# Cross attention on 32 batches: where the operand x is transposed, and how many operand tiles it uses

## The chip, the cores and the metric

One core of a Trainium2 chip runs the whole kernel. The metric is the device time of one execution in microseconds. Before the change the median of three runs is 336.96 us (336.56 to 337.16).

## The reference

Two layers run over 32 batches of x and y (the context), each 128 channels by 1024 positions.

```
# layer 0, per batch, 8 heads of 16 channels, softmax over a head's 16 channels
att(q, k, v) = v @ softmax(q.T @ k * 16**-0.5)            # per head, q, k, v are projections
x1 = x + y + proj_p2r @ att(wq_rgb x, wk_point y, wv_point y)
           + proj_r2p @ att(wq_point y, wk_rgb x, wv_rgb x)
# layer 1, per batch, 8 heads
q, k = Wq y + bq, Wk y + bk ;  v = Wv x1 + bv
o    = Wo (softmax(q k.T / sqrt(128)) v) + bo + x1        # attention between channels of a head
out  = (o - mean(o)) / sqrt(var(o) + 1e-5) * gn_w + gn_b  # mean and variance over the whole batch
```

All attention is between channels, so each batch needs only the 128x128 Gram matrices y y', y x' and the row sums of y; everything up to the normalisation is then one pair of 128x128 matrices P and Q with out = P x + Q y + shift.

## The kernel before, in words

The batches are taken in pairs (b = 0, 1); `h` counts two pairs, `u` is the pair in it, `p = 2h + u` is the number of the pair, and `slot = 2u + b` names one of four buffers. A batch passes three stages, and `step(h, u, front, middle, back, post)` does one stage each for three pairs: *front* builds the Gram of pair p, *middle* turns the Gram of pair p-1 into P and Q, *back* applies the P and Q of pair p-2 to its x and y, and *post* normalises pair p-3. `steps` calls it for 18 values of p: four by hand, twelve in a hardware loop of two steps (VectorE has its last two of these by hand), and the last two, one without front and one without front and middle. Each engine has its own list of calls in this step, and order on an engine is that of its list; semaphores alone tie the engines together.

Front. The operand tile `t` (four of them, `TB = 4`, one a slot) holds, for eight chunks of positions, y transposed (128 columns), a column of ones, and x transposed (128 columns). In the loop VectorE writes y from `y_blocks` by 32x32 block transposes (`y_transpose`, two halves a batch), and x of the second batch of a pair from `x_blocks` (`x_transpose` of VectorE). The x of the first batch is transposed by TensorE (`x_transpose` of PE, two groups of four into the banks `tpx`), and ScalarE copies it out (`xt_out`). The first four batches are all transposed on TensorE (`x_transpose_early`, `y_transpose_early`); ScalarE and VectorE copy them out. `gram_chunks` multiplies, ScalarE copies (`gram_out`), VectorE mirrors the part that was not computed (`gram_mirror`).

Middle. `u12_products` and `u3_products` multiply the Gram with key and query weights into `mid0` and `mid1`; ScalarE (`u12_out`, `keys_times_sums`) and VectorE (`u3_out`) copy out; `scores` fills six 32-column blocks of `mid0`; softmax alternates between VectorE (`shift_scores`, `softmax_out`) and ScalarE (`exponent`); `z_products`, `z_out` and `m_products` give `nmat` (`n12_out`, `n3_out` on VectorE), `pq_products` gives P and Q in `mid1`. Attention times bv is made in `softmax_out` by three VectorE operations and multiplied with Wo in `m_products` into two columns, from which `c_out` makes the shift. In the list of TensorE `pq_products(p - 2)` stands behind the first group of x transposes.

Back. The output product runs with split operands: `pq_hi` (ScalarE, `pq_high`) and `pq_lo` (VectorE, `pq_low`, from the bank and `pq_hi`), and `xy_hi` (ScalarE, `split_high`) and `xy_lo` (GpSimd, `split_low`, four pieces of 256 columns for x and for y). `out_half` sums hi*hi, hi*lo (parts 0) and lo*hi (parts 1) for x and y into `oacc`; ScalarE copies it out (`out_to_sbuf`), VectorE takes statistics (`half_stats`, `half_moments`, `partition_moments`, `variance`), TensorE averages over partitions (`group_moments`), GpSimd raises to the power -1/2 (`deviation`), ScalarE makes scale and shift and normalises (`norm_scale`, `normalise`), and issues the store. All loads are issued by SP, in its order: `refill_blocks` when both transposes of a batch are done, `refill_raw` when `xy_hi` and `xy_lo` are, each for the batch two pairs later.

In the last but one step ScalarE's list has the two `split_high` of the last batch, then `norm_scale(p - 3)`, and only then the first `out_to_sbuf`, and PE's product for the next use of `oacc` waits for that copy. `keep_warm` fills PE's pauses there with products that nobody reads.

Of the kernel before, what the change touches and what calls it, by code (L numbers as in the profile page):

```python
# [6 lines left out]
B, C, N, H = 32, 128, 1024, 8  # L7
EPS = 1e-5
# [4 lines left out]
QUADS = 4  # L13
# [4 lines left out]
TB = 4  # L18
# [6 lines left out]
VNAMES = ["bq", "bo", "gn_w", "gn_b"]  # L25


def cross_attention_pair_kernel(nc, x, y, weights, vectors, quad_rows, consts, out):
# [13 lines left out]
    with ctx:  # L42
# [14 lines left out]
        bk32, bv32 = quad[:, 0, :], quad[:, 1, :]  # L57
# [5 lines left out]
        zero_eps = cst[:, k0:k0 + 4]  # L63
# [5 lines left out]
        def col(name):  # L69
            k = VNAMES.index(name)  # L70
            return vec[:, k:k + 1]
# [5 lines left out]
        x_blocks = [sb(f"x_blocks{n}", [C, QUADS, N // QUADS]) for n in range(2)]  # L77
# [15 lines left out]
        abv_m = sb("abv_m", [C, 2, W32])  # L93
        square = sb("square", [C, 2])
        gmean = sb("gmean", [C, 2])
        gsquare = sb("gsquare", [C, 2])
        gvar = sb("gvar", [C, 2])
        abv = sb("abv", [C, 2])
# [4 lines left out]
        pq_lo = [sb(f"pq_lo{n}", [C, 2, 2, C], f32r) for n in range(2)]  # L103
        gate = sb("gate", [1, 10])
# [16 lines left out]
        sc = mid0[:, 0:6 * W32].rearrange("p (i c) -> p i c", c=W32)  # L121
        probs = mid0[:, 6 * W32:12 * W32].rearrange("p (i c) -> p i c", c=W32)
        stat_mb = stat[:, 0:4].rearrange("p (m b) -> p m b", b=2)
        pstat = stat[:, 8:12].rearrange("p (b m) -> p b m", m=2)
        mean_s, abv_s = stat[:, 16:18], mid0[:, 12 * W32:12 * W32 + 2]
        gacc_b = [gacc[:, 0:GW], stat[:, H64:H64 + GW]]
        oacc = [pb(f"oacc{n}", [C, HALF]) for n in range(2)]
        o_last = [oacc, [gacc, mid1]]
        y_early = [oacc, [mid0, mid1], oacc, oacc]
# [3 lines left out]
        weights_in = sem("weights_in")  # L133
        x_in = [sem(f"x_in{n}") for n in range(4)]
        y_in = [sem(f"y_in{n}") for n in range(4)]
        blocks_in = [sem(f"blocks_in{n}") for n in range(4)]
        x_blocks_in = [sem(f"x_blocks_in{n}") for n in range(2)]
# [3 lines left out]
        prepared = sem("prepared")  # L141
        attn_zero = sem("attn_zero")
# [23 lines left out]
        abv_step = sem("abv_step")  # L166
        abv_ready = sem("abv_ready")
# [5 lines left out]
        wo_abv_done = sem("wo_abv_done")  # L173
# [3 lines left out]
        pqhi_ready = sem("pqhi_ready")  # L177
        pqlo_ready = sem("pqlo_ready")
# [7 lines left out]
        square_ready = sem("square_ready")  # L186
# [4 lines left out]
        gvar_ready = sem("gvar_ready")  # L191
# [31 lines left out]
        def _(sp):  # L223
# [12 lines left out]
            def load_x_blocks(h, u):  # L236

                blocks = x[4 * h + 2 * u + 1].rearrange("(i c) (a m) -> a c i m", c=W32, a=QUADS)
                for a in range(QUADS):
                    sp.dma_start(x_blocks[u][W32 * a:W32 * (a + 1), :, :], blocks[a]).then_inc(x_blocks_in[u], 16)  # L240
# [14 lines left out]
            for n in range(2, 4):  # L255
                load_x(0, n)
                load_y(0, n)
# [940 lines left out]
```

## Time and profile before

| | |
|---|---|
| runs | 336.56, 336.96, 337.16 us |
| profiled execution | 336.94 us; its span, first to last instruction, 335.2 us |
| busy | PE 313.4, VectorE 263.8, ScalarE 231.2, GpSimd 190.4 us |
| moved | 56.8 MB read, 16.8 MB written |

The span is what the engines do; some 1.7 us of the time lie around it. Busy shares are averages over a start, thirteen alike steps and an end, so the stages have to be read one by one.

### The profile page before, as it was taken

How to read it: one execution, taken by the hardware profiler on the slowest of the kernel's cores; microseconds unless marked ns; L12 is line 12 of the kernel's file. 1: busy time of each engine (PE TensorE's matmuls, PEld its weight loads, DVE VectorE, ACT ScalarE, POOL GpSimd, SP SyncE). 2: the span in 40 equal slices, each digit the busy share in tenths (PEclk: the TensorE clock that was granted, in tenths of full speed). 3: DMA queues.
4: the chain of work that ended last, by engine and by line, in shares of the span. 5: the costliest groups of instructions: out<-in, count | busy, mean ns of one | idle time of the engine just before them, and what ended most of it. 6: DMA issues, size and time to landing. Idle time of an engine off the chain costs nothing.

```text
span 335.2 us, 12612 instructions
## 1 busy us (share of the span) xinstructions
PE 313.4 (94%) x4808; PEld 273.0 (81%) x4808; DVE 263.8 (79%) x716; ACT 231.2 (69%) x382; POOL 190.4 (57%) x277
## 2 busy tenths in 40 slices
PE   6999999999978999999999999999999999994980
PEld 3887898989866898988888898989898888972760
DVE  1595888988985788888898889888888999653574
ACT  3653757878785787878787797878787878954332
POOL 0874482757676275767667575757676675754010
PEclk9999999999999999999999999999999999997897
DMA  7999989498989949797998989797979670300215
GB/s 224 389 258 300 261 230 245 162 276 225 284 230 299 232 123 285 226 297 214 305 244 251 283 210 319 195 298 217 287 221 299 174 250 1 125 0 22 105 47 204
DMA packets 39061, 73.88 MB, mean 220 GB/s; under 512 B 4608, under 2 KB 26368, under 8 KB 39040
## 3 DMA queue, kind: packets, MB, share of 16 engines
q1 hardware_dynamic: 35008, 58.92, 64.6%
q10 hardware_dynamic: 4032, 14.68, 12.2%
q8 instruction: 13, 0.21, 0.3%
q14 instruction: 8, 0.07, 0.1%
HBM read 56.81 MB, written 16.78 MB: 220 GB/s over the span
## 4 chain that ended last, share of the span: by engine, by line
PE 88%; issue 3%; DVE 2%; POOL 2%; DMA 2%; ACT 2%; SPq 0%; POOLq 0%; ACTq 0%
PE oacc L429 10%; PE oacc L436 9%; PE oacc L430 9%; PE mid L526 5%; PE mid L454 4%; PE gacc L391 4%; PE mid L503 4%; PE stat L393 4%; PE tpx L348 4%; PE gacc L392 3%; PE gacc L393 3%; PE stat L392 3%; PE stat L391 3%; PE mid L512 2%; PE gacc L409 2%
## 5 line engine op out<-in xcount | busy, mean ns | idle before, releaser
L1129 POOL TENSOR_TENSOR xy_lo<-raw,xy_hi 128x256 fp32r<-128x256 f32 x256 | 179.9, 740 | 116.5 <-ACT xy_hi L696 116.5
L696 ACT ACTIVATE xy_hi<-raw 128x1024 fp32r<-128x1024 f32 x64 | 66.9, 1048 | 0.0
L856 DVE STREAM_TRANSPOSE t<-y_blocks 128x512 f32<-128x512 f32 x56 | 62.9, 1162 | 0.0
L429 PE MATMUL oacc<-xy_hi,pq_hi 128*128 128x512 f32 x124 | 55.6, 448 | 5.0 <-ACT res L703 4.8
L885 DVE BATCH_NORM_STATS2 hstat<-res 128x6 f32<-128x512 f32 x60 | 40.1, 688 | 22.8 <-ACT res L703 22.7
L703 ACT ACTIVATE res<-oacc 128x512 f32<-128x512 f32 x60 | 35.6, 594 | 30.7 <-PE oacc L436 30.4
L430 PE MATMUL oacc<-xy_lo,pq_hi 128*128 128x512 f32 x124 | 50.0, 403 | 1.5 <-issue 1.5
L394 PE MATMUL gacc<-t 128*32 128x225 f32 x224 | 45.4, 354 | 0.0
L393 PE MATMUL gacc<-t 128*32 128x225 f32 x224 | 45.4, 354 | 0.0
L394 PE MATMUL stat<-t 128*32 128x225 f32 x224 | 44.9, 353 | 0.0
L393 PE MATMUL stat<-t 128*32 128x225 f32 x224 | 44.9, 353 | 0.0
L391 PE MATMUL stat<-t 128*32 128x129 f32 x224 | 43.0, 272 | 1.8 <-issue 1.8
L392 PE MATMUL gacc<-t 128*32 128x161 f32 x224 | 44.2, 300 | 0.0
L392 PE MATMUL stat<-t 128*32 128x161 f32 x224 | 43.9, 299 | 0.0
L391 PE MATMUL gacc<-t 128*32 128x129 f32 x224 | 43.1, 273 | 0.4 <-issue 0.3
L436 PE MATMUL oacc<-xy_hi,pq_lo 128*128 128x512 f32 x124 | 40.9, 411 | 0.0
L717 ACT ACTIVATE res<-res,nbias,nscale 128x1024 f32<-128x1024 f32 x29 | 36.0, 1241 | 4.8 <-issue 4.3
L395 PE MATMUL stat<-t 128*32 128x96 f32 x224 | 36.8, 246 | 0.0
L395 PE MATMUL gacc<-t 128*32 128x96 f32 x224 | 36.8, 246 | 0.0
L429 PEld LDWEIGHTS oacc<-xy_hi,pq_hi 128*128 128x128 f32 x124 | 23.8, 192 | 12.8 <-issue 7.6
L866 DVE STREAM_TRANSPOSE t<-x_blocks 128x512 f32<-128x512 f32 x28 | 31.9, 1139 | 0.0
L396 PE MATMUL gacc<-t 128*32 128x64 f32 x224 | 30.8, 219 | 0.0
(146 smaller groups left out, 916.8 us busy)
## 6 DMA issues: line engine op xcount, KB each, us to landing
raw<-in_x SPq DMA_DIRECT2D x31, 512.0 KB, 5.7
raw<-in_ctx SPq DMA_DIRECT2D x31, 512.0 KB, 7.0
y_blocks<-in_ctx SPq DMA_DIRECT2D x112, 128.0 KB, 7.0
out<-res ACTq DMA_DIRECT2D x28, 512.0 KB, 3.4
x_blocks<-in_x SPq DMA_DIRECT2D x56, 128.0 KB, 6.7
out<-res SPq DMA_DIRECT2D x4, 512.0 KB, 2.8
wt<-in_weights SPq DMA_DIRECT2D x1, 896.0 KB, 7.0
raw<-in_x SPq DMA_DIRECT2D x2, 256.0 KB, 3.7
```

What stands on the lines that cost most here:

```text
L391: pe.matmul(acc[0:W32, C:GW], wa, tb[:, c, C:GW], start=first, stop=False)
L392: pe.matmul(acc[3 * W32:C, 3 * W32:GW], wd, tb[:, c, 3 * W32:GW], start=first, stop=False)
L393: pe.matmul(acc[W32:H64, W32:GW], wb, tb[:, c, W32:GW], start=first, stop=final)
L394: pe.matmul(acc[H64:3 * W32, W32:GW], wc, tb[:, c, W32:GW], start=first, stop=final)
L395: pe.matmul(acc[0:W32, 0:3 * W32], wa, tb[:, c, 0:3 * W32], start=False, stop=final)
L429: pe.matmul(bank[:, :], whi, xy_hi[slot][:, s, cols], start=(s == 0), stop=False)
L430: pe.matmul(bank[:, :], whi, xy_lo[slot][:, s, cols], start=False, stop=False)
L436: mm = pe.matmul(bank[:, :], pq_lo[u][:, b, s, :], xy_hi[slot][:, s, cols], start=False, stop=(s == 1))
L696: act.activation(xy_hi[slot][:, s, :], raw[slot][:, s, :], ACT.Copy).then_inc(split_hi, 1)
L856: dve.transpose(dst, blocks[:, HC * i:HC * (i + 1)]).then_inc(yt_ready, 1)
L885: dve.bn_stats(hstat[:, b, half, :], res[2 * u + b][:, half * HALF:(half + 1) * HALF])\
L1129: piece = pool.tensor_tensor(xy_lo[slot][:, s, cols], raw[slot][:, s, cols], xy_hi[slot][:, s, cols].bitcast(f32), ALU.subtract)
```

## The change

Every x of the loop is transposed by VectorE from `x_blocks` (now four tiles, loaded for every batch), and so is batch 3 at the start, x and y. Only two operand tiles are left, one for each b, so the halves of a batch's transposes spread around the mirror and into the next step. The TensorE banks `tpx` then hold u12, u3, the scores and the exponents, `mid` holds z, M and P, Q alone. The low parts of P and Q are made by GpSimd from SBUF, for which ScalarE copies the bank a second time (`pq_copy`). Attention times bv is no longer made on VectorE: z of Wo times bv are two one-column products. The chain of mean and variance is written in scalar-pointer forms. In the loop PE computes the high parts of both first halves ahead of the low parts. The last two steps have new lists on all engines: P and Q of the last pair are made one step earlier, ScalarE's scale of the older pair comes behind all copies, outputs go to four more banks, and `keep_warm` stands in one place only.

```diff
-TB = 4
+TB = 2
-        x_blocks = [sb(f"x_blocks{n}", ...) for n in range(2)]
+        x_blocks = [sb(f"x_blocks{n}", ...) for n in range(4)]
+        pq_full = sb("pq_full", [C, 2, 2, C])
+        tail = [tpx[i].rearrange("p m r -> p (m r)") for i in range(2)]
+        u12_bank, u3_bank = tail[0], tail[1][:, 0:2 * C]
+        sc = tail[1][:, 2 * C:2 * C + 6 * W32].rearrange("p (i c) -> p i c", c=W32)
+        probs = tail[0][:, 0:6 * W32].rearrange("p (i c) -> p i c", c=W32)
+        o_next = [oacc, [gacc, oacc[0]]]
+        o_last = [tail, [oacc[1], gacc]]
# SP
             def refill_blocks(h, u, b):
                 n = 4 * h + 2 * u + b
                 sp.wait_ge(yt_ready, 2 * n + 2)
                 load_blocks(h + 1, 2 * u + b)
-                if b == 1:
-                    sp.wait_ge(xt_ready[1], n + 1)
-                    load_x_blocks(h + 1, u)
+                sp.wait_ge(xt_ready[b], n - b + 2)
+                load_x_blocks(h + 1, 2 * u + b)
# TensorE, out_half
-                if half == 0 and b == 0:
-                    pe.wait_ge(pqlo_ready, 2 * h + u + 1)
+                if half == 0:
+                    pe.wait_ge(pqlo_ready, 2 * (2 * h + u) + b + 1)
# TensorE, z_operands
                 pe.wait_ge(attn_ready, p + 1)
+                if not (isinstance(p, int) and p < 1):
+                    pe.wait_ge(c_ready, p)
+                    pe.wait_ge(pq_copied, p)
# TensorE, m_products
-                pe.wait_ge(abv_ready, p + 1)
-                pe.matmul(mid0[:, 2 * C:2 * C + 2], w("oT"), abv[:, :], start=True, stop=True)
+                for a in range(2):
+                    mm = pe.matmul(mid0[:, 2 * C + a:2 * C + a + 1], z[:, a, 2, :],
+                                   (col("bv"), col("bv", vec_rot))[a], start=True, stop=True)
# TensorE, step in the loop
-                    x_transpose(h, u, 0)
                     pq_products(p - 2)
-                    x_transpose(h, u, 1)
                     u12_products(p - 1)
-                    out_half(h - 1, u, 0, 0)
                     u3_products(p - 1)
+                    out_half(h - 1, u, 0, 0, parts=(0,))
+                    out_half(h - 1, u, 0, 1, parts=(0,))
+                    out_half(h - 1, u, 0, 0, parts=(1,))
+                    out_half(h - 1, u, 0, 1, parts=(1,))
                     if post:
                         group_moments(p - 3)
-                    out_half(h - 1, u, 0, 1)
                     scores(p - 1)
# TensorE, last but one step (whole)
+                    u12_products(p - 1)
+                    u3_products(p - 1)
+                    pq_products(p - 2)
+                    scores(p - 1)
+                    out_half(h - 1, u, 0, 0, parts=(0,))
+                    out_half(h - 1, u, 0, 1, parts=(0,))
+                    out_half(h - 1, u, 0, 0, parts=(1,))
+                    out_half(h - 1, u, 0, 1, parts=(1,))
+                    z_operands(p - 1)
+                    keep_warm(1)
+                    z_products(p - 1)
+                    out_half(h - 1, u, 1, 0, banks=o_next, bank_free=0)
+                    group_moments(p - 3)
+                    m_products(p - 1, True)
+                    out_half(h - 1, u, 1, 1, parts=(0,), banks=o_next, bank_free=2 * n + 3)
+                    pq_products(p - 1)
+                    out_half(h - 1, u, 1, 1, parts=(1,), banks=o_next)
# ScalarE
+            def pq_copy(p):
+                if not (isinstance(p, int) and p < 1):
+                    act.wait_ge(pqlo_ready, 2 * p)
+                act.activation(pq_full[:, :, :, :], mid1[:, :], ACT.Copy).then_inc(pq_copied, 1)
# ScalarE, step in the loop (whole, "post" calls included)
+                    pq_high(p - 2, u)
+                    pq_copy(p - 2)
+                    u12_out(p - 1)
+                    keys_times_sums(p - 1)
+                    split_high(h - 1 + u, 1 - u, 1, 0, post)
+                    out_to_sbuf(h - 1, u, 0, 0)
+                    out_to_sbuf(h - 1, u, 0, 1)
+                    split_high(h - 1 + u, 1 - u, 1, 1, post)
+                    norm_scale(p - 3)
+                    exponent(p - 1)
+                    normalise(*before(h, u), 0)
+                    store(*before(h, u), 0)
+                    normalise(*before(h, u), 1)
+                    gram_out(p, 0)
+                    split_high(h, u, 0, 0, back)
+                    store(*before(h, u), 1)
+                    gram_out(p, 1)
+                    z_out(p - 1)
+                    split_high(h, u, 0, 1, back)
+                    out_to_sbuf(h - 1, u, 1, 0)
+                    out_to_sbuf(h - 1, u, 1, 1)
# ScalarE, last but one step (whole)
+                    u12_out(p - 1)
+                    keys_times_sums(p - 1)
+                    pq_high(p - 2, u)
+                    pq_copy(p - 2)
+                    split_high(h - 1, 1, 1, 0, True)
+                    exponent(p - 1)
+                    split_high(h - 1, 1, 1, 1, True)
+                    out_to_sbuf(h - 1, u, 0, 0)
+                    out_to_sbuf(h - 1, u, 0, 1)
+                    z_out_last(p - 1)
+                    out_to_sbuf(h - 1, u, 1, 0, o_next)
+                    pq_high(p - 1, 1 - u)
+                    pq_copy(p - 1)
+                    out_to_sbuf(h - 1, u, 1, 1, o_next)
+                    norm_scale(p - 3)
+                    normalise(*before(h, u), 0)
+                    store(*before(h, u), 0)
+                    normalise(*before(h, u), 1)
+                    store(*before(h, u), 1)
# ScalarE, last step (whole)
+                    norm_scale(p - 3)
+                    normalise(h - 1, 0, 0)
+                    normalise(h - 1, 0, 1)
+                    norm_scale(p - 2, slice(0, 1))
+                    normalise_last(h - 1, u, 0, range(2))
+                    normalise_last(h - 1, u, 1, range(1))
# VectorE, partition_moments and variance
+                for b in range(bs.start, bs.stop):
+                    mean = mom[:, 0, b:b + 1]
+                    last = dve.scalar_tensor_tensor(out=mom[:, 1, b:b + 1], in0=mean, scalar=mean,
+                                                    in1=pstat[:, b, 1:2], op0=ALU.mult, op1=ALU.add)
...
# VectorE, step in the loop (whole, "post" and "ahead" calls included)
+                    half_stats(*before(h, u), 1, 1)
+                    half_moments(p - 3)
+                    partition_moments(p - 3, 1 - u)
+                    u3_out(p - 1)
+                    x_transpose(h, u, 0, 1)
+                    y_transpose(h, u, 1, 0)
+                    x_transpose(h, u, 1, 0)
+                    variance(p - 3, 1 - u)
+                    shift_scores(p - 1)
+                    y_transpose(h, u, 1, 1)
+                    x_transpose(h, u, 1, 1)
+                    softmax_out(p - 1)
+                    half_stats(h - 1, u, 0, 0)
+                    half_stats(h - 1, u, 0, 1)
+                    y_transpose(h + u, 1 - u, 0, 0)
+                    x_transpose(h + u, 1 - u, 0, 0)
+                    gram_mirror(p)
+                    y_transpose(h + u, 1 - u, 0, 1)
+                    half_stats(h - 1, u, 1, 0)
+                    n12_out(p - 1)
+                    n3_out(p - 1)
+                    c_out(p - 1, 1 - u)
# GpSimd
+            def pq_low(p, parity):
+                pool.wait_ge(pqhi_ready, p + 1)
+                pool.wait_ge(pq_copied, p + 1)
+                for b in range(2):
+                    pool.tensor_tensor(pq_lo[parity][:, b, :, :], pq_full[:, b, :, :],
+                                       pq_hi[parity][:, b, :, :].bitcast(f32), ALU.subtract).then_inc(pqlo_ready, 1)
...
                 if middle and back:
+                    pq_low(p - 2, u)
                     split_low(h - 1 + u, 1 - u, 1, 0)
...
                 elif middle:
                     deviation(p - 3)
+                    pq_low(p - 1, 1 - u)
                     deviation(p - 2)
```

In the last step VectorE's variance of the last batch still waits for `norm_ready`, which ScalarE's `norm_scale(p - 2, slice(0, 1))` now raises.

## Rows read from the trace of the kernel before

**Rows 1.** The page: span, busy time and share by engine.
```profile
span 335.2 us, 12612 instructions
...
PE 313.4 (94%) x4808; PEld 273.0 (81%) x4808; DVE 263.8 (79%) x716; ACT 231.2 (69%) x382; POOL 190.4 (57%) x277
```

**Rows 2.** Windows (stretch, length, busy by engine, granted clock, DMA share, GB/s).
```profile
184.35:202.73 18.38, 18.38 (x317) 16.41 (x316) 16.22 (x43) 14.46 (x24) 11.85 (x18) 1.00 0.95 260
20.00:40.00 20.00, 19.70 (x211) 16.53 (x213) 14.50 (x32) 11.83 (x20) 8.63 (x14) 1.00 1.09 276
302.30:307.00 4.70, 0.00 (x0) 0.00 (x0) 0.07 (x1) 1.54 (x5) 3.09 (x5) 0.93 0.00 0
307.00:322.00 15.00, 14.42 (x85) 11.63 (x86) 9.60 (x33) 5.62 (x9) 0.03 (x1) 0.79 0.18 71
```

**Rows 3.** Timeline of VectorE in one pair: start, length, instruction, idle before it.
```profile
164.31 0.69 DVE L885 BATCH_NORM_STATS2 hstat<-res 128x6 f32<-128x512 f32 x1 [0.26 <-ACT res L703]
...
168.37 0.68 DVE L878 TENSOR_TENSOR pq_lo<-mid,pq_hi 128x512 fp32r<-128x512 f32 x1
168.97 2.28 DVE L856 STREAM_TRANSPOSE t<-y_blocks 128x512 f32<-128x512 f32 x2
...
172.50 1.12 DVE L866 STREAM_TRANSPOSE t<-x_blocks 128x512 f32<-128x512 f32 x1
...
176.54 0.36 DVE L981 TENSOR_REDUCE ssum<-mid 128x6 f32<-128x192 f32 x1 [0.81 <-ACT mid L659]
```

**Rows 4.** Timeline of the end: rows of GpSimd, PE and VectorE.
```profile
299.18 5.56 POOL L1129 TENSOR_TENSOR xy_lo<-raw,xy_hi 128x256 fp32r<-128x256 f32 x8 [4.11 <-ACT xy_hi L696]
...
307.04 0.77 PE L429 MATMUL oacc<-xy_hi,pq_hi 128*128 128x512 f32 x1 [4.78 <-ACT res L703]
...
317.47 1.16 PE L526 MATMUL mid<-nmat 128*128 128x128 f32 x8
...
316.99 0.42 DVE L1011 TENSOR_TENSOR nmat<-mid,cst 128x256 f32<-128x256 f32 x1
...
331.21 0.81 DVE L950 TENSOR_SCALAR res<-mid,nscale,nbias 128x512 f32<-128x512 f32 x1
```

**Rows 5.** Timeline of PE in one pair.
```profile
165.26 0.28 PE L517 MATMUL mid<-abv,wt 128*128 128x2 f32 x2
...
165.95 0.60 PE L348 MATMUL tpx<-cst,raw 128*128 128x128 f32 x4
166.39 1.06 PE L526 MATMUL mid<-nmat 128*128 128x128 f32 x8
...
167.72 1.03 PE L454 MATMUL mid<-wt,gram 128*128 128x256 f32 x4
168.42 0.57 PE L429 MATMUL oacc<-xy_hi,pq_hi 128*128 128x512 f32 x1
...
169.98 0.61 PE L463 MATMUL mid<-wt,gram 128*128 128x128 f32 x4
```

**Rows 6.** One line's instructions (min, median, max ns), and VectorE's timeline at the start.
```profile
L989 DVE TENSOR_TENSOR sinv<-sinv,own_half x16: 159/161/661, 25.3 to 309.7; 128x12 f32<-128x12 f32 x16
...
14.51 0.22 DVE L827 TENSOR_SCALAR wt<-wt 128x128 f32<-128x128 f32 x1
14.64 0.76 DVE L828 TENSOR_SCALAR wt<-wt 128x128 f32<-128x128 f32 x1
```

**Rows 7.** Timeline of GpSimd in the same pair.
```profile
179.11 1.44 POOL L1129 TENSOR_TENSOR xy_lo<-raw,xy_hi 128x256 fp32r<-128x256 f32 x2 [2.41 <-ACT xy_hi L696]
```

**Rows 8.** Windows of one microsecond each, columns as in rows 2, and issues to landing.
```profile
192.00:193.00 1.00, 1.00 (x40) 1.00 (x33) 0.93 (x5) 0.54 (x2) 1.00 (x3) 1.00 1.13 184
201.00:202.00 1.00, 1.00 (x8) 0.92 (x7) 0.90 (x2) 0.06 (x1) 1.00 (x3) 1.00 1.01 407
...
x_blocks<-in_x SPq DMA_DIRECT2D x56, 128.0 KB, 6.7
```

**Rows 9.** Timeline of PE: one of the two places where it waits for instructions.
```profile
107.96 0.50 PE L430 MATMUL oacc<-xy_lo,pq_hi 128*128 128x512 f32 x1 [1.54 <-issue]
```

More of the change, by code:

```diff
@@ L136, in cross_attention_pair_kernel @@
         blocks_in = [sem(f"blocks_in{n}") for n in range(4)]
-        x_blocks_in = [sem(f"x_blocks_in{n}") for n in range(2)]
+        x_blocks_in = [sem(f"x_blocks_in{n}") for n in range(4)]
         x_half_in = [sem(f"x_half_in{n}") for n in range(2)]
@@ L254, in _ @@
             sp.dma_start(w_rot[H64:C, :, :], weights[0:H64, k:k + 2, :]).then_inc(weights_in, 16)
[L255 to L257 removed]
+            load_x(0, 2)
+            load_y(0, 2)
+            sp.dma_start(vec_rot[0:H64, :], vectors[H64:C, :]).then_inc(weights_in, 16)
+            sp.dma_start(vec_rot[H64:C, :], vectors[0:H64, :]).then_inc(weights_in, 16)
+            load_blocks(0, 3)
+            load_x_blocks(0, 3)
             load_blocks(1, 0)
+            load_x_blocks(1, 0)
+            load_x(0, 3)
+            load_y(0, 3)
             load_blocks(1, 1)
[L260 removed]
+            load_x_blocks(1, 1)
             def raw_free(h, u, b):
@@ L408, in gram_full_width, with out_half @@
                 for c in range(begin, end):
-                    mm = pe.matmul(gacc_b[b], t[n][:, c, 0:C], t[n][:, c, :], start=(c == 0), stop=(c == CH - 1))
+                    mm = pe.matmul(gacc_b[b], t[b][:, c, 0:C], t[b][:, c, :], start=(c == 0), stop=(c == CH - 1))
                 if end == CH:
                     mm.then_inc(gram_done, 1)
-            def out_half(h, u, b, half, last=False, parts=range(2)):
-                bank = o_last[b][half] if last else oacc[half]
+            def out_half(h, u, b, half, parts=range(2), banks=(oacc, oacc), bank_free=None):
+                bank = banks[b][half]
                 slot = 2 * u + b
@@ L424, in out_half @@
                         pe.wait_ge(split_lo, 2 * n + 2)
-                    if not (last and b == 1):
+                    if bank_free is None:
                         pe.wait_ge(o_out, 2 * n + 1 + half)
+                    elif bank_free:
+                        pe.wait_ge(o_out, bank_free)
                     for s in range(2):
@@ L820, in _, with prepare_mask, prepare_weights @@
             dve.wait_ge(attn_zero, 2 * QUADS)
-            def prepare():
+            def prepare_mask():
+                s1 = float(C) ** -0.5
                 dve.wait_ge(consts_in, 16)
-                dve.wait_ge(weights_in, 80)
+                dve.wait_ge(small_in, 32)
+                dve.tensor_scalar(nbq[:, :], col("bq"), s1 * N, None, ALU.mult).then_inc(mask_ready, 1)
+                dve.tensor_copy(mask6[:, 0:4, :], other_head.unsqueeze(1).broadcast_to([C, 4, W32]))
+                dve.wait_ge(mask_ready, 1)
+                for a in range(2):
+                    last = dve.scalar_tensor_tensor(out=mask6[:, 4 + a, :], in0=bk32, scalar=nbq[:, :],
+                                                    in1=other_head, op0=ALU.mult, op1=ALU.add)
+                last.then_inc(mask_ready, 1)
+            def prepare_weights():
+                dve.wait_ge(weights_in, 16 * 5)
                 s0, s1 = float(C // H) ** -0.5, float(C) ** -0.5
@@ L1022, in step @@
                 if front and not middle:
-                    for b in range(2):
-                        for i in range(2):
-                            y_early_out(b, i)
-                    prepare()
+                    y_early_out(0, 0)
+                    y_early_out(0, 1)
+                    prepare_mask()
+                    y_early_out(1, 0)
+                    y_early_out(1, 1)
+                    prepare_weights()
                     gram_mirror(p)
```

285 lines of the change are left out of this document (100 added, 185 removed).

## The prediction

> **What bounds the kernel now.** I read the page first: TensorE is busy 94% of a 335.2 us span, VectorE 79% [rows 1]. Then the stretches: one pair of batches in the loop takes 18.38 us (18.40 in the pair before), with PE busy for all of it at the full granted clock (1.00, the 2.4 GHz level), VectorE 16.2, ScalarE 14.5, GpSimd 11.9 and a DMA share of 0.95 [rows 2]. So in the loop the bound is TensorE. The timeline of VectorE shows three idle pieces in a pair, from 0.26 to 0.81 us, 1.65 in all [rows 3], so it is occupied for 18.40 - 1.65 = 16.75. It is the next bound, 1.65 behind. The third view is the end: for 4.7 us PE does nothing, and in the 15 us after it the granted clock is 0.79 [rows 2]. PE waits there for a copy of ScalarE into res, which is queued behind the scale of an older pair, which waits for GpSimd's power, which stands behind 5.56 us of low parts [rows 4].
>
> **The change, part by part.** Times are of the profiled execution: 335.2 us span, 336.94 us run, so 1.74 us lie around the span; the median of the runs is 336.96, the same.
>
> PE, per pair in the loop. Two groups of four transposes of x go, 166.39 - 165.95 = 0.44 each, 0.88 together. The 2-column product (0.14, 165.26 to 165.40) becomes two products: +0.14. The first two output halves run in one row and switch once less: about -0.15 (the first product after a change of kind takes 0.57 where the others take 0.40) [rows 5]. PE needs 18.40 - 0.88 + 0.14 - 0.15 = 17.5.
>
> VectorE, per pair. It gains two transposes of x: one takes 1.12, of which the next instruction overlaps 0.08, so about +2.10. It loses the low part of P and Q, 0.60 (168.37 to 168.97). The mean and variance chain loses two operations and two waits, about -0.35. No trace shows the new scalar-pointer forms on two values; the nearest two-value operations are 0.07 apart without a wait and 0.19 with one, so the pair of them lies between 0 and +0.25; I take the first. The three operations for bv cost 0.10 of the softmax, since the chain sum, reciprocal, scale paces it [rows 3]. Trimmed of the ends of instructions that now overlap the next (six, 0.08 each) VectorE needs 16.75 + 2.10 - 0.60 - 0.35 - 0.10 - 0.50 = 17.3.
>
> But VectorE and PE now wait for each other in a ring. Before, x transposes stood in front of the P and Q products and covered the wait for nmat. Now: the last nmat addition starts, 0.48 later the first P/Q product runs (316.99 to 317.47 [rows 4]); 0.89 + 0.70 + 0.65 = 2.24 after that u3's product has landed (166.39, 167.72, then 0.65 as 169.98 to its reader) [rows 5]. In these 2.72 us VectorE has only 1.84 of work (end of nmat and shift 0.47, the last statistics 0.73, moments 0.31, partition moments 0.33) and idles for 0.88. From u3_out to the last nmat addition it has 15.4 without a pause: u3_out 0.48, eight transposes 8.6, variance 0.60, scores 1.04, softmax 1.3, three statistics 1.8, mirror 0.97, first nmat addition 0.64. Ring: 2.72 + 15.4 = 18.14. PE's 17.5 is inside it with 0.6 to spare, so TensorE stops being the bound and most of the 0.88 is lost.
>
> One more term. The scale of the softmax, two SBUF inputs, took 0.16 in most pairs and 0.66 in a few; the same 128x128 scaling took 0.22 in front of GpSimd's low parts and 0.76 beside them [rows 6]. In the loop it fell into GpSimd's pause (176.70 to 179.11 [rows 7]). Now GpSimd's second block of four low parts starts about 1.4 later in the pair, because the new low parts of P and Q (two of 0.74, as the 128x256 form of the page) and the later deviation precede it; it ends 10.5 us after the P/Q products, and the scale comes at 10.3. Bounds 0 to +0.5, I take +0.2. The Trainium skill (SBUF — State Buffer, "SBUF: two separate sides") says that GpSimd and a VectorE operation with two SBUF inputs exclude each other for a whole instruction, while a one-input operation doesn't wait. By that rule the transposes stay at their price, which the trace agrees with (1.07 to 1.22 us), and the scale pays up to one GpSimd piece; by a rule that made every VectorE operation wait, the pair would be over 20 us.
> So a pair takes 18.14 + 0.2 = **18.34**, against 18.40.
>
> ScalarE loses two copies of 0.49 and gains one of 0.50; it finishes z about 15.0 after the P/Q products, and PE asks at 15.1. Near, but PE has 0.6 in hand. The low parts of P and Q are ready at 3.0 (high copy 1.1 to 1.6, second copy to 2.2, GpSimd 0.74), and PE, with the high products of both halves first, asks at 4.0. Cost 0; without that order PE would wait about 0.4. Two operand tiles: t[0] is rewritten after this pair's first Gram (done at 8.8; VectorE comes at 12.2), t[1] for the pair itself at 4 to 9.7, needed at 10.4. Cost 0, with 0.6 of cover on the second.
>
> DMA: each pair loads 0.52 MB more in 1 KB runs. A microsecond with blocks alone moved 184 GB/s, one of raw or stores 407 [rows 8]: 0.52 / 0.184 = 2.85 us more on about 16.3 busy, 19.1 in all against 18.34. But loads are issued two pairs ahead and land in 7 us [rows 8]: some 20 us of lead, of which 12 pairs would use 12 x 0.8 = 10. I take 0; the bounds are 0 and, with no lead, +0.8 a pair.
>
> Start. Four early transposes groups of batch 3 (1.75 on PE) go, but its two x and two y transposes (4.3) stand on VectorE between softmax steps. By its durations the second half of batch 3 is ready at 28.7; then z 0.8, the Gram's rest 1.4 and the copy of z: the P/Q products start at 34.15, against 33.62 now: +0.5. Step to the next one: 52.0 against 52.3.
> Loop. Twelve pairs: 52.0 + 12 x 18.34 = 272.1. PE stood twice for instructions, about 1.8 and 2.0 us [rows 9], once in the run; of these 3.8 the cover of 0.9 hides part: +2.9. That makes 275.0, against 276.9: **-1.9**. Last full step: 17.5 against 18.0: **-0.5**.
>
> End. From the end of that step E (now 294.92) the span has 40.3 us left. In the new order nothing stands in front of the copies: u12, u3 and P/Q to 2.2, scores 2.9, the two halves to 5.9, z at 6.2 (softmax of the last pair done at 6.0), out and M to 10.1, last P/Q 11.9, high copy 12.7, second copy 13.2, low part 13.95; last outputs to 19.0. With no idle piece over 0.5 us PE keeps 2.4 GHz: the products that took 0.43 take 0.23. Then ScalarE is last: copy to 13.7, scale 14.7, two normalisations with stores 17.6, scale 19.0, two more 21.4 (1.24 each), scale of the last pair 22.2; VectorE's variance of the last batch waits for that, 0.4 + 0.82 + 0.50 to the last normalisation at 23.9; from there to the end 4.0 (331.21 to 335.2) [rows 4]. 27.9 in all: **-12.4**.
>
> Sum: -1.9 - 0.5 - 12.4 = -14.8; span 320.4, time **322**.
>
> **Rivals.**
> A longer ring. All eight transposes at their longest (1.22) beside GpSimd and the full 0.5 for the scale: 18.95 a pair, 12 x 0.6 = +7: **329**. For it: GpSimd is busier now. Against: one-input operations show little spread.
> A shorter ring. The trimmed durations are too long or the u3 wait is met earlier, and PE stays the bound at 17.6 to 17.7: 12 x -0.7 = -8: **314**. For it: VectorE's own work is 17.3. Against: the 2.24 us are three products in a row.
> The end gains half. Some copy on ScalarE holds PE, the clock falls to 1.2 GHz again, and 6 of the 12.4 come back: **328**. For it: it is one queue with 12 long activations. Against: GpSimd's power no longer has anything behind it that PE needs.
> The DMA queues decide, on the other side. Place: the loop; 0.95 x 18.38 = 17.5 engine-us a pair plus 2.85 x 1.13 = 3.2 make 20.7 at a share of 1.0. If the lead doesn't carry it, 12 x 2.4 = +28: **350**, slower. It decides from 18.34 + 14.9/12 = 19.6 a pair. Against: 20 us with mixed loads ran at a share of 1.09 [rows 2].
>
> **How the numbers follow.** Forecast 0.55 (its own range 317 to 327), longer ring 0.16, shorter ring 0.12, half the end 0.12, DMA 0.05. The range 314 to 329 leaves out about 2 in 10. A difference of 0.2% (0.7 us) is about what runs of this kernel can tell. Faster: all but the DMA case and a sliver of unlucky sums, 0.93; same 0.02; slower 0.05.
>
> **What would show it.** PE idle about 0.9 us in each pair, just before the P/Q products, released by nmat on VectorE; pair period 18.2 to 18.5; VectorE busy near 17.3 with one idle piece before u3_out; the softmax scale at 0.3 or more; in the end no PE idle piece over 1 us before 305, clock at its full level to the last products, and ScalarE's scale as the releaser of the last variance. A PE without idle in the loop, or raw and blocks awaited by ScalarE or VectorE, would make me wrong there.

## The result: slower, 341.6 us against 336.8

After the change the median of four runs is 341.6 us (340.1 to 343.3); the kernel before, run beside it, took 336.8 (336.05 to 337.16). The ratio is 1.0147, 95% interval [1.0084, 1.021]: slower by 0.8 to 2.1%. Some executions of any of these kernels are a few per cent longer at a lower granted clock; the medians in this document are of all runs, the ratios leave those executions out. The profiled execution took 340.34 us with a span of 338.3, where the prediction had 322 and 320.4: 17.9 us of span are to be explained.

The page of the kernel after (answers to [rows 1]; then slices of 8.5 us, granted clock and DMA share in tenths; then the loads and the instruction fetches by queue):

```profile
span 338.3 us, 12492 instructions
...
PE 304.0 (90%) x4696; PEld 262.1 (77%) x4696; DVE 277.9 (82%) x671; ACT 226.3 (67%) x371; POOL 214.3 (63%) x309
...
PEclk9999997989999999999999999999999999999996
DMA  7999999997889987999999999999999994311036
...
q1 hardware_dynamic: 44384, 67.32, 73.8%
...
q8 instruction: 12, 0.20, 0.3%
```

PE was busy 9.4 us less and the span grew by 3.1. The clock dips in slices 7 and 9, in the first steps, and no longer between 302 and 322 us, where it had dipped before [rows 2]; it falls again only in the last slice, when PE has almost nothing left to do. A yardstick for the place of the loss is the start of the last nmat addition, once a step, here in us (before, line 1011; after, line 1002):

| | 1st | 2nd | 3rd | 4th | 5th | 14th | 15th | span end |
|---|---|---|---|---|---|---|---|---|
| before | 33.14 | 51.58 | 69.79 | 88.21 | 110.46 | 276.01 | 294.44 | 335.2 |
| after | 34.30 | 58.64 | 81.80 | 100.62 | 122.21 | 290.80 | 309.48 | 338.3 |

From row to row: the start +1.2; the first four steps 87.9 instead of 77.3, +10.6; nine steady steps 168.6 (18.73 each) instead of 165.55 (18.39), +3.0; the last full step +0.25; the end 28.8 instead of 40.8, -11.9. Together +3.1.

**The first steps.** PE's timeline of the kernel after, the three longest waits for which the profile names no releaser ("issue"), as in [rows 9]:

```profile
52.11 1.09 PE L494 MATMUL mid<-wt,attn 64*64 64x128 f32 x17 [4.14 <-issue]
...
72.97 0.37 PE L381 MATMUL stat<-t 128*32 128x96 f32 x1 [3.30 <-issue]
...
114.86 0.35 PE L380 MATMUL stat<-t 128*32 128x225 f32 x1 [2.99 <-issue]
```

Windows of the same kernel, columns as in [rows 2]:

```profile
52.00:56.00 4.00, 3.89 (x24) 3.02 (x24) 0.00 (x0) 2.68 (x4) 0.00 (x0) 0.57 1.12 236
...
50.00:60.00 10.00, 7.88 (x48) 6.30 (x48) 3.14 (x6) 3.87 (x5) 2.81 (x4) 0.83 1.08 262
...
70.00:80.00 10.00, 7.03 (x88) 6.23 (x89) 6.04 (x11) 5.48 (x8) 2.80 (x4) 0.83 1.07 337
```

With 1.37 and 0.48 us earlier, PE stood 12.3 us in such waits between 20 and 122 us; in the kernel before 3.6. Around the waits at 52 and 73 us the granted clock falls from 2.4 to 1.2 GHz: 0.57 in the row 52:56 means 3.4 of the 4 us at the lower level. It doesn't fall behind the wait of 2.99 us. No engine covers such a gap: VectorE is busy 3.14 us of ten.

What PE waits for can be read from the trace's DMA packets. The instruction queue q8 moves 12 packets of 16 KB in the run (0.20 MB by the page), and one belongs to each long wait:

| PE stands | packet begins | packet has landed | PE goes on | landing to going on |
|---|---|---|---|---|
| 47.97 | 49.43 | 50.51 | 52.11 | 1.60 |
| 69.67 | 70.22 | 71.66 | 72.97 | 1.31 |
| 111.87 | 112.06 | 113.38 | 114.86 | 1.48 |

In each row the packet begins only after PE has stopped. The 13 profiles of this document hold 51 such waits of 0.3 us or more between 40 and 122 us, and all of them end 1.21 to 1.61 us after such a packet has landed. So PE waits for its next code. The packets themselves take 1.1 to 1.4 us in these three rows, no longer than others that nobody waits for; it is their start that comes late, and the records don't say what held it. Between 118.6 and 312.3 us, when the loop's code has been passed once, q8 moves no packet and no such wait is left.

The wait of 1.37 us is another matter. It stands in every version of the changed kernel (1.09 to 1.37), no packet times it, and it ends 0.10 us after VectorE's transpose of batch 3's x, which the change brought:

```profile
27.86 1.09 DVE L871 STREAM_TRANSPOSE t<-x_blocks 128x512 f32<-128x512 f32 x1
29.05 0.67 PE L395 MATMUL stat<-t 128*128 128x257 f32 x2 [1.37 <-issue]
```

That leaves 10.9 us of waits for code, against 3.6.

**A steady step.** PE and VectorE in one pair (answers to [rows 5] and [rows 3]; start, length, instruction, idle before it):

```profile
197.58 1.16 PE L518 MATMUL mid<-nmat 128*128 128x128 f32 x8 [0.80 <-DVE nmat L1002]
198.58 1.03 PE L444 MATMUL tpx<-wt,gram 128*128 128x256 f32 x4
199.44 0.61 PE L451 MATMUL tpx<-wt,gram 128*128 128x128 f32 x4
```

```profile
197.10 0.43 DVE L1002 TENSOR_TENSOR nmat<-mid,cst 128x256 f32<-128x256 f32 x1
...
200.09 0.61 DVE L958 SCALAR_TENSOR_TENSOR u<-wt,gram,tpx 128x128 f32<-128x128 f32 x2 [0.85 <-PE tpx L451]
...
203.84 0.14 DVE L916 COPY gmean<-stat 128x2 f32<-128x2 f32 x1
...
204.01 0.34 DVE L921 SCALAR_TENSOR_TENSOR gsquare<-stat,gmean,cst 128x1 f32<-128x1 f32 x2
...
204.66 0.35 DVE L968 TENSOR_TENSOR tpx<-tpx,mask 128x192 f32<-128x192 f32 x1
...
208.40 0.17 DVE L982 TENSOR_TENSOR sinv<-sinv,own_half 128x12 f32<-128x12 f32 x1
...
215.85 0.43 DVE L1002 TENSOR_TENSOR nmat<-mid,cst 128x256 f32<-128x256 f32 x1
```

PE's 0.80 and VectorE's 0.85 are the only idle pieces of the ring, and the waits of the whole run (us in total, times, longest) show them in every step:

```profile
PEld mid L518 <- DVE nmat L1002: 14.8, 14, 1.3
...
DVE u L958 <- PE tpx L451: 10.3, 14, 0.9
```

One turn of the ring is 197.10 to 200.09, 2.99 us, the leg on PE, and 200.09 to 215.85, 15.76, the leg on VectorE. The scale of the softmax over the whole run (count, then min, median, max ns), which answers to the first row of [rows 6]:

```profile
L982 DVE TENSOR_TENSOR sinv<-sinv,own_half x16: 170/172/490, 27.2 to 314.4; 128x12 f32<-128x12 f32 x16
```

In the pair shown GpSimd's block of low parts ran from 205.47 to 208.30, and the next one began at 211.10: the scale, at 208.40, came 0.10 us behind the block. No low part runs beside any of the 15 short ones. The one of 490 ns, at 314.36, met a piece that ran from 314.08 to 314.83, and ended 0.03 us behind it.

**The end.** A window where PE had stood still [rows 2], and VectorE's last rows:

```profile
302.30:307.00 4.70, 4.70 (x79) 3.98 (x73) 2.71 (x8) 4.67 (x7) 2.17 (x4) 1.00 0.55 223
```

```profile
332.43 0.15 DVE L918 TENSOR_TENSOR cmu<-cshift,stat 128x1 f32<-128x1 f32 x1 [0.65 <-ACT nbias L642]
...
334.14 0.81 DVE L951 TENSOR_SCALAR res<-gacc,nscale,nbias 128x512 f32<-128x512 f32 x1
```

### The profile page after: what moved, and what is told of

It is laid out like the page before. It is cut to its first block, busy times and chain, and to the rows that moved or that the text cites. A ratio compares the mean times of both kernels' runs of the same rounds, so it can differ in the third digit from the quotient of the medians.

```text
span 338.3 us, 12492 instructions
## 1 busy us (share of the span) xinstructions
PE 304.0 (90%) x4696; PEld 262.1 (77%) x4696; DVE 277.9 (82%) x671; ACT 226.3 (67%) x371; POOL 214.3 (63%) x309
## 3 DMA queue, kind: packets, MB, share of 16 engines
HBM read 65.20 MB, written 16.78 MB: 242 GB/s over the span
## 4 chain that ended last, share of the span: by engine, by line
DVE 47%; PE 32%; issue 11%; ACT 3%; DMA 2%; SPq 2%; DVEq 1%; POOL 0%; POOLq 0%; ACTq 0%
DVE t L860 13%; DVE t L871 13%; PE mid L518 5%; PE tpx L444 4%; DVE hstat L884 4%; DVE gram L878 3%; DMA vec_rot<-in_vectors 2%; PE oacc L417 2%; PE oacc L418 2%; PE tpx L451 2%; PE oacc L424 2%; PE mid L494 2%; DVE nmat L994 2%; DVE nmat L1002 1%; DVE u L958 1%
## 5 line engine op out<-in xcount | busy, mean ns | idle before, releaser
L871 DVE STREAM_TRANSPOSE t<-x_blocks 128x512 f32<-128x512 f32 x58 | 66.8, 1151 | 0.0
L860 DVE STREAM_TRANSPOSE t<-y_blocks 128x512 f32<-128x512 f32 x58 | 66.3, 1143 | 0.4
L417 PE MATMUL oacc<-xy_hi,pq_hi 128*128 128x512 f32 x120 | 50.8, 423 | 0.1
L701 ACT ACTIVATE res<-oacc 128x512 f32<-128x512 f32 x59 | 33.6, 597 | 25.0 <-PE oacc L424 24.6
L380 PE MATMUL stat<-t 128*32 128x225 f32 x224 | 46.9, 362 | 3.0 <-issue 3.0
L418 PE MATMUL oacc<-xy_lo,pq_hi 128*128 128x512 f32 x120 | 47.8, 399 | 0.0
L379 PE MATMUL stat<-t 128*32 128x225 f32 x224 | 46.9, 362 | 0.0
L1132 POOL TENSOR_TENSOR pq_lo<-pq_full,pq_hi 128x256 fp32r<-128x256 f32 x32 | 23.1, 744 | 36.5 <-ACT pq_full L673 36.5
L378 PE MATMUL stat<-t 128*32 128x161 f32 x224 | 45.3, 305 | 0.0
L424 PE MATMUL oacc<-xy_hi,pq_lo 128*128 128x512 f32 x120 | 36.9, 409 | 0.0
L382 PE MATMUL stat<-t 128*32 128x64 f32 x224 | 31.5, 223 | 0.0
```

What stands on the lines that cost most here:

```text
L378: pe.matmul(acc[3 * W32:C, 3 * W32:GW], wd, tb[:, c, 3 * W32:GW], start=first, stop=False)
L379: pe.matmul(acc[W32:H64, W32:GW], wb, tb[:, c, W32:GW], start=first, stop=final)
L380: pe.matmul(acc[H64:3 * W32, W32:GW], wc, tb[:, c, W32:GW], start=first, stop=final)
L417: pe.matmul(bank[:, :], whi, xy_hi[slot][:, s, cols], start=(s == 0), stop=False)
L418: pe.matmul(bank[:, :], whi, xy_lo[slot][:, s, cols], start=False, stop=False)
L860: dve.transpose(dst, blocks[:, HC * i:HC * (i + 1)]).then_inc(yt_ready, 1)
```

## The experiments

The theories. A: the added loads fill the DMA queues in the first 80 us, and PE's code comes late behind them. B: the ring of VectorE and PE costs the loop 0.33 a step. C: the new end gives 11 to 12 us by itself. D, against parts of B: an order of the ring that is shorter on paper makes another engine wait. Where an expectation counts PE's waits for instructions in the changed kernel (12.2 us), it takes the 1.37 us of the start for one of them.

**1. The loads without the change.**

```diff
+ x_unread = sb("x_unread", [C, QUADS, N // QUADS])      # in the kernel before
+ if b == 0: load_unread(h + 1, u)                       # in refill_blocks
+ load_blocks(0, 3); load_x_blocks(0, 1)                 # at the start, as in the change
...
```

> The kernel before with the changed kernel's DMA traffic and nothing else: the x blocks of every first batch (0.52 MB a pair, 1 KB runs) and the blocks of batch 3 are loaded into a tile that nothing reads; the lists of all compute engines stay. Theory A (PE's instruction fetches are late because the data queues keep the 16 DMA engines full): PE shows issue waits of 3 us and more in its first 120 us and loses 4 to 10 us more than the 3.8 of before; time 341 to 347. Rival B (the longer waits come from PE's new list alone, whose fetches fall at other places): 336 to 338. Rival C (data loads are late): x_in, y_in or blocks_in appear as releasers of ScalarE or VectorE, time above 345.

Measured: runs of 348.82, 352.82, 355.17 and 523.16 us, ratio by the first two 1.0378 [1.0148, 1.0608]. The profile is of the third (span 353.4). It read the same 65.20 MB as the kernel after. PE's list is that of the kernel before, and its waits for code are now (sum, times, longest):

```profile
PE stat L412 <- issue: 4.4, 1, 4.4
PE stat L411 <- issue: 3.7, 1, 3.7
PE stat L415 <- issue: 3.0, 1, 3.0
```

11.1 us against 3.6, first four steps 94.9 against 77.3, and from then on 18.42 a step, as before, with PE busy 169.97 of 170 us at a DMA share of 0.99. Loads that nobody reads make the kernel slower, only at the start, and by more than the 341 to 347 of A. The waits for code are 7.5 of the 17.5 us that the four steps grew. PE also stood 2.70 us for data, which is rival C's sign, as is a time above 345:

```profile
36.70 0.81 PE L368 MATMUL tpx<-cst,raw 128*128 128x128 f32 x4 [2.70 <-DMA raw<-in_x]
```

And the granted clock was at its lower level for 17.1 us in four stretches, which by an estimate costs half of that, 8.5 us. So A is right in direction, but here it is less than half of the loss. The changed kernel has no such wait for data behind 20 us.

**2 and 3. The change with fewer bytes**, all along for two of four batches (light_loads), or only for batches 3 to 7 (light_early): the x blocks are loaded at a quarter of their bytes, and the rest of the tile is zero, so that part of x is left out of the Gram.

```diff
- sp.dma_start(x_blocks[n][W32 * a:W32 * (a + 1), :, :], blocks[a])
+ sp.dma_start(x_blocks[n][W32 * a:W32 * (a + 1), 0:k, :], blocks[a][:, 0:k, :])   # k = 1
```

> The changed kernel with the loads of the x blocks of first batches cut to a quarter of their bytes (the rest of the tile is zero, so that part of x is left out of the Gram). PE's list is that of the changed kernel. Theory A: the issue waits of 4.1, 3.3 and 3.0 us in the first 120 us shrink to under 2 each with the clock dips behind them, period still 18.75, time 329 to 334. Rival B: the waits stay, time 340 to 342.

> The changed kernel with the x blocks of batches 3 to 7 alone cut to a quarter of their bytes (2 MB less by 50 us; the rest of those tiles is zero); all later loads whole. Theory A with a backlog (the data queues are behind only because of the start): the waits at 52 and 73 us fall under 2, that at 115 goes too, time 333 to 336. Theory A without (any fetch beside full queues is late): the wait at 52 shrinks, that at 73 or 115 stays at 3 us, time 335 to 339. Rival B (not the loads): 340 to 342.

Measured: 334.03 us, ratio 0.9889 [0.9739, 1.004], and 332.13, ratio 0.9836 [0.9766, 0.9905]; both intervals lie below that of the change (1.0084 to 1.021). The first is at the top of its 329 to 334, the second a little below its 333 to 336. Windows of light_early:

```profile
50.00:60.00 10.00, 9.68 (x54) 8.06 (x52) 7.15 (x17) 7.10 (x12) 5.03 (x8) 1.00 0.83 215
60.00:70.00 10.00, 9.69 (x266) 8.84 (x265) 9.69 (x22) 8.34 (x14) 7.32 (x11) 1.00 0.84 202
```

PE's waits for code fall to 5.4 and 5.3 us, the longest 2.64 and 1.72, the first four steps take 81.3 and 79.9, and in light_early the clock stays at 1.00. Taking 2.0 MB (five times three quarters of 0.52) off loads issued before 32 us is worth as much as taking bytes off the whole run. The step in the loop stays at 18.77 and 18.72: DMA isn't the bound there.

**4. Same bytes, issued later.** Block loads of a pair behind its Grams.

```diff
- sp.wait_ge(yt_ready, 2 * n + 2)
+ if b == 0: sp.wait_ge(gram_done, n + 2)
+ else: sp.wait_ge(yt_ready, 2 * n + 2)
...
+ sp.wait_ge(gram_done, 3)     # ahead of the blocks of batch 6; 4 ahead of those of batch 7
...
```

> The changed kernel with the same loads in the same order, but SP holds the y and x blocks back longer: the block loads of the first batch of a pair are issued behind both Grams of that pair instead of behind its own transposes, those of batches 6 and 7 behind the Grams of batches 2 and 3. Everything SP issues behind them comes later too, by about 6 to 15 us; it still leads its use by more than one pair. The bytes are the same. Backlog theory (a fetch of PE's instructions queues behind loads that are far ahead of use): DMA share in 30 to 60 us falls from 1.08-1.11 to 1.0 or less, PE's waits for instructions go from 12.2 us to under 6, 333 to 337 us. Rival (it is the volume, not its place: whatever is held back has to be moved later, and PE's fetches meet it there): waits of 10 us or more somewhere before 120 us, 339 to 343. Second rival (less lead, so engines wait for data): rows of ScalarE or VectorE that wait for a DMA, 342 or more.

Measured: 340.12 us, ratio 1.0123 [1.0005, 1.024]: the rival's number (339 to 343), and not to be told from the change's 1.0147. PE's waits for code are 8.4 us, the first four steps 85.6. Windows:

```profile
40.00:50.00 10.00, 8.05 (x242) 7.08 (x241) 9.61 (x17) 4.06 (x7) 7.86 (x12) 1.00 1.08 261
50.00:60.00 10.00, 6.98 (x41) 5.44 (x40) 3.39 (x7) 3.27 (x4) 3.06 (x5) 0.83 0.85 239
...
70.00:80.00 10.00, 9.29 (x129) 7.72 (x121) 9.50 (x22) 7.02 (x11) 6.41 (x10) 1.00 0.75 223
```

Holding back works where it reaches: at 70 to 80 us the share is 0.75 and the 3.30 us wait has gone, though one of 2.11 has come at 95 us. Until 50 us the share is still 1.08, and the wait at 53 us (3.59) is still there. The volume that the first 50 us need by themselves fills the queues; so the rival has the larger half, and I had put too much on the lead.

**5 and 6. The order in the ring.** ring_open puts the u12 and u3 products ahead of P and Q, on ScalarE likewise; ring_u3_behind takes u12, P and Q, u3.

```diff
-                    pq_products(p - 2)
                     u12_products(p - 1)
+                    pq_products(p - 2)      # ring_u3_behind; behind u3_products in ring_open
                     u3_products(p - 1)
```

> The changed kernel with PE's u12 and u3 products ahead of the P and Q products in the loop steps, and ScalarE's copies in that order. Theory (ring of VectorE and PE): VectorE's wait for u3 of 0.9 us a pair goes, the period falls from 18.75 to 17.9 (VectorE's own work), 13 pairs: -11 us, time 329 to 333. Rival D (VectorE alone is the bound, and waits elsewhere instead): period 18.5 to 18.75, time 338 to 342.

> The changed kernel, loop steps: u12's products into PE's idle time ahead of P and Q, u3's products behind them, so that they cover part of the wait for the high copy; ScalarE copies u12, then P and Q twice, then makes the key sums. Theory (the ring is one dependence, u3 behind P and Q): VectorE waits 0.1 to 0.3 us for u3, PE 0.4 for the high copy, period 18.2 to 18.4, time 335 to 338. Rival D (VectorE's own 17.9 us plus a new wait of the same size): period 18.7 to 18.9 as when u3 stood ahead too, time 340 to 345.

Measured: ring_open 345.23 us, ratio 1.023 [1.0097, 1.0363], step 18.89; ring_u3_behind 339.96, ratio 1.0074 [1.0029, 1.0119], step 18.43. PE's first output product in a pair, in ring_open and in ring_u3_behind:

```profile
202.64 0.50 PE L417 MATMUL oacc<-xy_hi,pq_hi 128*128 128x512 f32 x1 [0.98 <-ACT pq_hi L668]
```

```profile
201.14 0.49 PE L417 MATMUL oacc<-xy_hi,pq_hi 128*128 128x512 f32 x1 [0.56 <-ACT pq_hi L668]
```

ring_open missed my number by some 14 us, and D's by 3: the wait moved from VectorE to PE, which now stands 0.98 us for P and Q's copy on ScalarE. That is the kind of thing D said, at a higher price. With half of the move the step is 0.30 shorter than in the change, and no better than before: VectorE is then occupied for all but 0.41 us of it (two waits of 0.18 and 0.23 on ScalarE's copies). Its time, 339.96, falls between the 335 to 338 expected and D's 340 to 345, and doesn't separate it from the change (intervals [1.0029, 1.0119] and [1.0084, 1.021]); the shorter step is shown by the profile, which had 11.5 us of waits for code.

**7 and 8. Both cures together**: u3 behind, with light loads or with the paced ones.

> Both causes taken away: u3 behind P and Q, and the x blocks of first batches at a quarter of their bytes (part of x left out). If the two account for the miss, 332 (light loads) less 13 pairs of 0.4: 326 to 328. If something else bounds the loop at 18.75: 332.

> The same pacing on the variant with the u3 product and its copies behind P and Q (pair period 18.44 instead of 18.75; 340.0 us without pacing). If backlog and ring add up: 339.96 - 6 = 332 to 335. If the gain of the ring meets the waits again, 336 to 340.

Measured: 334.04 us, ratio 0.9856 [0.9769, 0.9943], step 18.44, PE's waits for code 8.7 us, with one of 3.32 at 51 us; and 336.9 us, ratio 0.9931 [0.9871, 0.9992], step 18.44, waits 9.1 us. The first is outside both of its numbers (326 to 328, and 332), the second in the range for a gain that meets the waits again (336 to 340). The shorter step (12 x 0.30 = 3.6) came in both. With paced loads it shows, 336.9 against 340.1 us; with light ones PE's waits grew by 3.3 over light_loads and took it back. Kernels that differ only in the order of the loop differ by 3.3 us in these waits at the same loads (8.2 in ring_open, 11.5 in ring_u3_behind), and that part I can't forecast. This is the best version of the changed loop with all its bytes, and still behind the old loop with the new end, below.

**9 to 11. The end by itself.** tail_alone moves only ScalarE's scale, normalisations and stores of the older pair behind the copies, in the last-but-one step of the kernel before. new_end_old_loop gives the kernel before the whole last two steps of the change (banks, order, P and Q of the last pair one step earlier, low parts still on VectorE). paced_new_end adds experiment 4's edit.

```diff
-                    norm_scale(p - 3)
                     out_to_sbuf(h - 1, u, 0, 0)
...
                     z_out_last(p - 1)
+                    norm_scale(p - 3)
+                    normalise(*before(h, u), 0)
...
```

> The kernel before with one part of the change's idea for the end alone: in the last but one step ScalarE scales and normalises the older pair behind all copies. Theory E (the end's gain is the 4.8 us wait and the halved clock after it): the wait is under 1 us, the granted clock stays 1.00 to 320, time 327 to 331. Rival F (half of it comes back, since z_out_last and the last scale now queue behind each other on ScalarE): 331 to 335.

> The kernel before with the last two steps of the change (lists, banks, P and Q of the last pair one step early) and nothing of its loop, its start or its loads; the low parts stay on VectorE. If the end is worth what the changed trace shows (28.8 us from the last but one nmat to the end of the span, against 40.8): -12, time 324 to 326 beside 337. Rival F (the end needs the changed loop's lighter PE list or GpSimd's low parts to be worth it): 328 to 332.

> The same pacing on the kernel before with the change's last two steps (326.8 us, PE's waits for instructions 7.0 us in all). If the backlog is behind these waits too: 3 to 5 us of them go, 322 to 324. If the waits at 104 and 112 us, at a DMA share of 0.94, stay (3.3 us) and only those at 44 and 50 go: 324. If pacing does nothing here: 326 to 327.

Measured: tail_alone 332.18 us, ratio 0.9811 [0.9674, 0.9949], in rival F's range; its end is 33.6 instead of 40.8. new_end_old_loop **326.81 us**, ratio 0.9674 [0.962, 0.9728], end 29.6: faster than both kernels, and C holds, a little short of the 324 to 326 expected. paced_new_end 327.38, ratio 0.9663 [0.9576, 0.975]: no difference from it that can be told, so the 3 to 5 us that pacing should have brought didn't show in the time, though its profile has 4.5 us of PE's waits instead of 7.0.

What each profile had; the waits are those between 20 and 122 us, without the one that batch 3's transpose explains:

| kernel | DMA share 40 to 80 us | PE's waits for code, us | first four steps, us | steady step, us |
|---|---|---|---|---|
| before | 0.87 | 3.6 | 77.3 | 18.40 |
| after | 1.08 | 10.9 | 87.9 | 18.73 |
| unread_loads | 1.08 | 11.1 | 94.9 | 18.42 |
| light_early | 0.94 | 5.3 | 79.9 | 18.72 |
| light_loads | 1.01 | 5.4 | 81.3 | 18.77 |
| paced_loads | 0.89 | 8.4 | 85.6 | 18.73 |
| ring_open | 1.05 | 8.2 | 89.3 | 18.89 |
| ring_u3_behind | 1.08 | 11.5 | 89.1 | 18.43 |
| light_and_u3_behind | 1.01 | 8.7 | 84.5 | 18.44 |
| paced_u3_behind | 0.93 | 9.1 | 84.8 | 18.44 |
| tail_alone | 0.74 | 7.6 | 83.8 | 18.48 |
| new_end_old_loop | 0.84 | 7.0 | 82.3 | 18.39 |
| paced_new_end | 0.72 | 4.5 | 78.2 | 18.39 |

The last three have PE's old code in these stretches and no more loads than the kernel before. So 4 to 8 us of such waits belong to that code and those loads in any case, and I predicted from the profile with the fewest, 3.6; its time, 336.94 us, was an ordinary one. One profile a kernel is thin evidence for any single row. In the changed loop the waits are fewer where early bytes were taken away (5.3, 5.4 and 8.7) than where all of them were there (8.2 to 11.5), with some overlap. The share over 40 us doesn't order the rows: tail_alone has 7.6 at 0.74, before 3.6 at 0.87.

## Why the prediction was wrong

By its own steps; the miss is 17.9 us of span.

- **The failing step: the DMA term, "I take 0; the bounds are 0 and, with no lead, +0.8 a pair".** It asked only whether data would come late. None did (no load of x or y blocks is awaited anywhere; the lead was enough, as worked out). What came late was PE's own code. The 3.8 us of waits in [rows 9] was carried over as 2.9, as if independent of the loads. Measured: the first step 24.3 instead of 17.85 (+6.5), and the twelve steps of the loop 232.2, which is 7.4 above twelve steady ones of 18.73, instead of 2.9 (+4.5). The first step's +6.5 is 4.6 us of waits for code (0.48 and 4.14) and an estimated 1.7 us of the lower clock. Of the two together, +11.0, light_early gave 8.0 back in the first four steps with early bytes alone.
- **The DMA rival had the wrong mechanism and place.** It priced 28 us over the loop from an exhausted lead. In fact the loop ran at a share of 1.02 in the pair shown (0.97 from 122 to 290 us) without a late load, and the loss lay ahead of 122 us. A chance of 0.05 for the only rival of the other sign was too small given that 20 to 40 us already stood at 1.09 [rows 2].
- **The ring, right in mechanism, short by 0.39 a pair (+4.7).** (In the pair shown 0.41.) PE's idle 0.80 before the P and Q products and VectorE's 0.85 before u3_out are as forecast (0.9 and 0.88). The leg on PE is 2.99, not 2.72: P and Q 1.00 and u12 0.86 from start to start, where [rows 5] gave 0.89 and 0.70 in another neighbourhood. VectorE's leg is 15.76, not 15.42, and 0.22 of that is the variance: a copy, a subtraction and four scalar-pointer operations take 203.84 to 204.66, 0.82, forecast 0.60. The prediction left the price of the new forms between 0 and +0.25 and took 0; the trace has the upper end. Line 921 takes 0.34 for the two batches in two operations, where one operation on both (line 920 of the kernel before, at 171.84) took 0.16, and the old chain of the variance, 171.64 to 172.50, took 0.86: the new forms saved 0.04. The transposes were right: eight of them 8.6.
- **The scale beside GpSimd: +0.2 forecast, 0 measured, by 0.1 us of luck.** The forecast had the scale start 0.2 before GpSimd's block ended (10.3 and 10.5 after the P and Q products); it started 0.10 after (10.8 and 10.7). The one scale that did meet a low part took 0.49 instead of 0.17. So the other terms of the ring fell short by 0.6.
- **PE's own 17.5 and last full step 17.5.** PE was busy 17.90 in a pair, 0.48 less than before and not 0.9, and the last full step took 18.68: the ring held there too (+1.2).
- **Start: 34.15 forecast, 34.78 measured (+0.6).** VectorE waited 3.0 and 2.0 us for two small tensors (vec_rot, quad), where in the kernel before it waited for no load at all, and the last transpose of batch 3 ended at 30.93, forecast 28.7; what each of these added isn't separated.
- **The end: -12.4 forecast, -11.9 measured.** PE is without an idle piece from 302.3 to 307, the clock is full there, and the last variance is released by ScalarE, each as written. new_end_old_loop shows the same end without the rest of the change. Here the method, following each queue row by row, worked.

The Trainium skill (Runtime: NRT & Kernel Launch, "Instruction fetch mechanics") says that each sequencer fetches its code in 16 KiB blocks through a DMA queue of its own while it runs the block before, and that the cost is mostly hidden. The 12 packets with 0.20 MB in the profile agree with the size; "mostly hidden" doesn't hold here, with 10.9 us of PE's waits for code.

Open: what decides whether a given fetch begins in time or late enough to hold PE for 4 us. More early traffic makes the sum of the waits grow on the whole; a single one it doesn't explain. paced_new_end still has a wait of 3.14 us at 104 us, in microseconds with DMA shares of 1.01, 0.72 and 0.66, and experiment 7 has more of them than experiment 2 at the same loads.

## What to carry to other kernels

A high DMA share (1.08 to 1.12 over 20 us and more in these profiles) can be a cost even if all data are early, as long as an engine still runs code for the first time: count the waits marked "issue" in the profile before, check that a packet of the instruction queue lands just before each ends, and price added traffic there first. One that no packet times may be a wait for another engine. Work moved from a bound engine to the next one needs the round trip between the two summed, not each engine's load: here TensorE's busy time fell by 0.48 us a pair and the step grew by 0.33. And an edit that combines a good end with a bad loop should be taken apart: the end alone was worth 3.3%.

## What the runs showed of the hardware

- With traffic that nobody reads, PE's waits for code rose from 3.6 to 11.1 us. A loop whose code had been passed once had none, at a DMA share of 0.99 there and of 0.97 in the change.
- In 13 profiles, 51 waits of PE without a releaser ended 1.21 to 1.61 us after a 16 KB packet of the instruction queue had landed. In the three longest of the change the packet took 1.1 to 1.4 us and began 0.2 to 1.5 us after PE had stopped.
- Around the waits of 4.14 and 3.30 us PE's granted clock fell to the 1.2 GHz level (0.57 over four microseconds), which by an estimate added 4 x 0.43 = 1.7 us to each; around the one of 2.99 us it stayed at 1.00.
- Two scalar-pointer operations on one column each took 0.34 us together (line 921, x2), and one operation on both columns 0.16; the chain of the variance took 0.82 in the new form and 0.86 in the old.
- A 128x12 product with two SBUF inputs took 0.17 us in 15 pairs, in each of which no low part of GpSimd ran beside it, and 0.49 in the one where it met a low part; it ended 0.03 us behind that low part. In the kernel before the two long ones, 0.65 and 0.66 us, each ended 0.03 us behind such a piece too.
